# A selective state-space layer and a 34-expert feed-forward on one core: the loop rotated by three pairs, and the state-space work cut into half chunks

## The reference, cut to what matters

```python
# state-space layer, per batch; DI = 256 channels, DS = 16 states, L = 256 positions
x = einsum('ed,bld->bel', in_proj_w, hidden_states)      # hidden_states is ctx, 128 wide
u = silu(conv4(x) + conv_b)                               # causal convolution, 4 taps
x_dbl = einsum('ke,bel->bkl', x_proj_w, u)                # 8 rows dt_lo, 16 rows B, 16 rows C
delta = softplus(dt_proj_w @ dt_lo + dt_proj_b)
for t in range(L):
    state = state * exp(delta_t * A) + (delta_t * u_t) * B_t   # 256 channels x 16 states
    y_t = sum_n(state * C_t)
y = (y + D * u) * silu(z)                                 # z: the layer-normed input

# residual, layer norm, then the experts
probs = softmax(flat @ router_w + router_b); topk = top_k(probs, 6)
out = mean over 2 shared experts  of  relu(x @ w1 + b1) @ w2 + b2
    + sum over 32 routed experts of gate * (relu(x @ w1 + b1) @ w2 + b2)
```

## Time and profile before

| | |
|---|---|
| Median of 3 runs | 467.87 us (465.32 to 468.52) |
| The profiled execution's own time | 467.62 us |
| Its span, first to last instruction | 465.8 us |
| PE busy | 392.7 us (84%) |
| PEld busy | 345.1 us (74%) |
| DVE busy | 331.1 us (71%) |
| ACT busy | 244.6 us (53%) |
| POOL busy | 156.6 us (34%) |
| Chain that ended last, by engine | PE 52%, DVE 22%, issue 19%, ACT 4% |
| Mean granted TensorE clock | 0.952 of full speed |

### The profile page before, as it was taken

One profiled execution on the slowest core, in us unless ns is written; L12 is line 12 of the kernel. 1 busy time (PEld: TensorE's weight loads), 2 busy tenths in 40 slices (PEclk: granted clock), 3 DMA queues, 4 the chain that ended last, 5 costly groups with the idle time before them and its releaser, 6 DMA issues.

```text
span 465.8 us, 7761 instructions
## 1 busy us (share of the span) xinstructions
PE 392.7 (84%) x2610; PEld 345.1 (74%) x2610; DVE 331.1 (71%) x570; ACT 244.6 (53%) x536; POOL 156.6 (34%) x115
## 2 busy tenths in 40 slices
PE   1547655999777999899779999998879999999996
PEld 1225434888667898788668897887768998999996
DVE  3499965769999655579999565489999575444443
ACT  5565611884563252864553343856453445655662
POOL 0454440301455421202464321202465312444442
PEclk9998775899999999899998999899989999999999
DMA  5333483022121213122121224112212222332220
GB/s 187 90 90 97 131 225 149 23 52 83 49 69 39 77 58 113 52 60 68 45 68 45 68 59 125 52 48 65 61 52 67 58 66 91 90 91 78 85 68 24
DMA packets 18872, 36.29 MB, mean 78 GB/s; under 512 B 2082, under 2 KB 4898, under 8 KB 18756
## 3 DMA queue, kind: packets, MB, share of 16 engines
q1 hardware_dynamic: 18852, 36.04, 26.5%
HBM read 34.98 MB, written 1.05 MB: 77 GB/s over the span
## 4 chain that ended last, share of the span: by engine, by line
PE 52%; DVE 22%; issue 19%; ACT 4%; DVEq 1%; DMA 1%; SPq 0%; ACTq 0%
PE acc L401 22%; PE z L421 7%; DVE bu L659 7%; PE z L423 6%; PE z L422 6%; DVE bu L665 3%; DVE stage L739 3%; PE gb L430 3%; DVE pr L675 3%; DVE hl L751 1%; PE bb L340 1%; PE misc L335 1%; DVE cv L605 1%; PE cc L331 1%; PE misc L366 1%
## 5 line engine op out<-in xcount | busy, mean ns | idle before, releaser
L557 ACT ACTIVATE stage<-z,par 128x256 f32<-128x256 f32 x188 | 78.9, 470 | 143.8 <-PE z L423 143.7
L421 PE MATMUL z<-xh,w1l 128*128 (+1 forms) x376 | 116.9, 311 | 6.3 <-DVE stage L741 3.6
L808 POOL TENSOR_TENSOR w2l<-w,w2h 128x512 fp32r<-128x512 f32 (+1 forms) x51 | 68.8, 1351 | 143.2 <-ACT w2h L564 143.2
L423 PE MATMUL z<-xh,w1h 128*128 (+1 forms) x376 | 107.9, 287 | 0.0
L422 PE MATMUL z<-xl,w1h 128*128 (+1 forms) x376 | 107.8, 287 | 0.0
L739 DVE TENSOR_TENSOR stage<-stage,gb 128x512 f32<-128x512 f32 x88 | 59.9, 683 | 66.3 <-ACT stage L557 66.2
L790 POOL TENSOR_TENSOR ya<-ya,pr 128x512 f32<-128x512 f32 x42 | 55.6, 1346 | 120.6 <-DVE pr L675 120.6
L665 DVE TENSOR_TENSOR_SCAN bu<-dA,bu 128x512 f32<-128x512 f32 x64 | 81.3, 1310 | 3.4
L401 PE MATMUL acc<-stage,w 128*128 128x256 f32 x348 | 82.1, 379 | 0.0
L421 PEld LDWEIGHTS z<-xh,w1l 128*128 128x128 f32 x376 | 72.8, 194 | 11.5 <-DVE stage L741 4.7
L422 PEld LDWEIGHTS z<-xl,w1h 128*128 128x128 f32 x376 | 73.0, 194 | 0.8
(11 more groups left out here) (117 smaller groups left out, 512.8 us busy)
## 6 DMA issues: line engine op xcount, KB each, us to landing
w<-in_w SPq DMA_DIRECT2D x92, 256.0 KB, 2.7
stage<-in_w SPq DMA_DIRECT2D x11, 512.0 KB, 3.6
selg<-in_selg SPq DMA_DIRECT2D x1, 1056.0 KB, 8.4
x<-in_xT SPq DMA_DIRECT2D x4, 256.0 KB, 4.4
out<-x SPq DMA_DIRECT2D x4, 256.0 KB, 2.6
xr<-in_xr SPq DMA_DIRECT2D x1, 768.0 KB, 10.2
w<-in_w SPq DMA_DIRECT2D x4, 128.0 KB, 2.1
stage<-in_w SPq DMA_DIRECT2D x1, 384.0 KB, 4.2
```

The lines of the kernel that those rows point to most:

```text
L421: pe.matmul(z[p % 2][:, i, :], w1l[:, t, one], xh_, start=k == 0, stop=False)
L423: mm = pe.matmul(z[p % 2][:, i, :], w1h[:, t, one], xh_, start=False, stop=k == KD - 1)
L557: ins = act.activation(hg[:, p % 4, i, :], z[p % 2][:, i, :], ACT.Relu, bias=b1[:, t:t + 1])
L808: pool.tensor_tensor(w2l[:, p % 4, 0:n, :], w2[:, p % RING, 0:n, :], w2h[:, p % 4, 0:n, :].bitcast(F32), ALU.subtract).then_inc(S["w2l_don ...
```

## The change

The loop is rotated: one iteration now runs pairs 3 to 23 of batch i and then pairs 0 to 2 of batch i+1, so that the second layers of pairs 21 to 23 stand beside pairs 0 to 2 of the next batch. The loop has two iterations; the third such stretch and the last batch are written out. Each chunk is cut into two half chunks, one for each half k of the channels, one at each of the pairs 0 to 15, and the fold of a half chunk goes with it. The gate of z is spread over pairs 2 to 10. The steps ahead of the chunks are made for batch i+2, at pairs 14 to 23. The products for dt, B and C become one (`xall`). The second bias product moves to pair 4 (`B2_AT`). `SPLIT` has 12 pairs where it had 9, and now holds for batch 0 too. Scratch tiles are reassigned.

```diff
-CHUNKS = [(("chunk", c), at) for c, at in enumerate([6, 8, 9, 10, 11, 13, 14, 15])]
-FRONT = [("xin", 0), ("cv0", 0), ("stats", 0), ("taps", 0), ("rs1", 1), ("econv", 1), ("nb1", 1), ("uclip", 1),
-         ("usig", 3), ("u", 3), ("xdt", 4), ("dtl", 4), ("zsig", 3), ("zmul", 5), ("dt", 5), ("xbc", 5), ("split", 5), ("sp", 5),
-         ("delta", 5)]
-BACK = [("x1", 17), ("mean", 19), ("centre", 19), ("var", 20), ("r2", 20), ("norm", 21), ("xh", 23), ("logits", 23),
-        ("xl", 23), ("top", 23), ("ex", 23), ("gates", 23)]
-SPLIT = [0, 2, 3, 11, 12, 14, 19, 20, 21]
+UNITS = []
+for _c in range(NC):
+    UNITS += [(("B", _c), 2 * _c), (("C", _c), 2 * _c + 1)]
+    for _k in range(KD):
+        _u = 2 * _c + _k
+        UNITS += [(("decay", _c, _k), max(_u - 1, 0)), (("bu", _c, _k), _u), (("scan", _c, _k), _u),
+                  (("prod", _c, _k), _u), (("fold", _c, _k), _u)]
+ZGATE = [("stats", 2), ("rs1", 3), ("nb1", 4), ("zz", 5), ("ez1", 6), ("ez2", 7), ("ez3", 8), ("zmul", 10)]
+BACK = [("yfold", 16), ("x1", 17), ("mean", 18), ("centre", 18), ("var", 19), ("r2", 19), ("norm", 20), ("logits", 21),
+        ("xl", 21), ("top", 21), ("ex", 22), ("gates", 22)]
+NEXT = [("xin", 14), ("cv0", 15), ("taps", 16), ("econv", 17), ("uclip", 17), ("usig", 18), ("u", 19), ("xall", 20),
+        ("dtl", 20), ("split", 20), ("dt", 21), ("sp", 21), ("delta", 23)]
+OPEN = [[("xall", 1), ("dtl", 1), ("split", 1)], [("dt", 1), ("sp", 1), ("delta", 1)],
+        [(n, 1) for q in range(SKEW) for n, at in THIS if at == q]]
+SPLIT = [2, 4, 6, 8, 10, 12, 14, 17, 18, 19, 21, 22]
...
+            def beside(b, p, this=True, later=True):
+                return ([(n, b + 1) for n, at in THIS if this and at == p] +
+                        [(n, b + 2) for n, at in NEXT if later and at == p])
+
+            for name, b in HEAD:
+                step(name, b)
+            for p in range(SKEW):
+                pair(0, p, OPEN[p])
+            with eng.Fori(0, B - 2) as i:
+                for p in range(SKEW, NP):
+                    pair(i, p, beside(i, p))
+                for p in range(SKEW):
+                    pair(i + 1, p, beside(i + 1, p))
+                final(i)
...
+                elif name == "xall":
...
+                    for k in range(KD):
+                        mm = pe.matmul(cc[0:NXA, 0, :], xall[:, k, :], u[:, k, :], start=k == 0, stop=k == KD - 1)
...
+                elif name[0] == "bu":
+                    c, k = name[1:]
+                    if c == 0:
+                        dve.wait_ge(S["delta_done"], b + 1)
+                    else:
+                        dve.wait_ge(S["prod_done"], (b * NC + c - 1) * KD + k + 1)
+                    dve.wait_ge(S["b_ready"], b * NC + c + 1)
+                    dve.tensor_tensor(bu[:, k, :].rearrange("p (j l) -> p j l", j=2), bb[:],
+                                      du[:, k:k + 1, :].broadcast_to([P, 2, L]), ALU.mult).then_inc(S["bu_done"], 1)
+                elif name[0] == "scan":
+                    c, k = name[1:]
+                    nth = (b * NC + c) * KD + k + 1
+                    dve.wait_ge(S["bu_done"], nth)
+                    dve.wait_ge(S["da_ready"], nth)
+                    dve.tensor_tensor_scan(bu[:, k, :], dA[:, k, :], bu[:, k, :], 0.0, ALU.mult,
+                                           ALU.add).then_inc(S["scan_done"], 1)
```

More of the change, by code:

```diff
@@ L26 @@
 NC = NS // 2
+NBC = 3 * 2 * NS
+NXA = NBC + DR
 EPS = 1e-5
@@ L433, in pair @@
                     turn(b)
-                if more:
-                    beside(p, b_step, b + 1)
-                if p >= SKEW:
-                    second_layer(b, p - SKEW)
-                if more:
-                    beside(p, step, b + 1)
-            def end(b):
-                for p in range(NP - SKEW, NP):
-                    second_layer(b, p)
-            def b_then_step(name, b):
-                b_step(name, b)
-                step(name, b)
-            run(pe, pair, end, b_then_step)
+                for name, at in beside:
+                    step(name, at)
+                if exists(b, p, SKEW):
+                    second_layer(*before(b, p, SKEW))
+            run(pe, pair, nothing, step)
+            for p in range(NP - SKEW, NP):
+                second_layer(B - 1, p)
         @block.scalar
         def _(act):
-            me = Steps(act, act_step, 7)
+            fr, zs = Steps(act, act_front_step, 3), Steps(act, act_z_step, 3)
             act.preload_act_table_set("natural_log_exp_and_others")
@@ L550, in step, with pair @@
                     ins.then_inc(S["ex_done"], 1)
-            def pair(b, p, more):
-                if first("pair", b) or p == 0:
+            def pair(b, p, beside):
+                if first(b) and p < SKEW:
                     act.wait_ge(w1l_done, NW)
@@ L575, in upper_h @@
                 act.activation(hh[:, p % 4, 0:n], hg[:, p % 4, 0:n], ACT.Copy).then_inc(S["hh_done"], 1)
-            def end(b):
-                if split(b, NP - 1):
-                    upper_h(b, NP - 1)
-            run(act, pair, end, step)
+            run(act, pair, nothing, step)
+            upper_h(B - 1, NP - 1)
         @block.vector
         def _(dve):
-            me, own = Steps(dve, dve_step, 19), Steps(dve, dve_router_step, 15)
+            fr, zs = Steps(dve, dve_front_step, 8), Steps(dve, dve_z_step, 2)
+            bk, own = Steps(dve, dve_back_step, 8), Steps(dve, dve_router_step, 15)
             dve.memset(epsc[:], EPS).then_inc(const_done, 1)
@@ L742, in pair @@
                 ins.then_inc(S["hg_done"], 1)
-                if p and split(b, p - 1):
-                    lower_h(b, p - 1)
-                if more:
-                    beside(p, step, b + 1)
+                if exists(b, p, 1) and split(*before(b, p, 1)):
+                    lower_h(*before(b, p, 1))
+                for name, at in beside:
+                    step(name, at)
             def lower_h(b, p):
@@ L752, in lower_h, with final @@
                                   ALU.subtract).then_inc(S["hl_done"], 1)
-            def end(b):
-                if split(b, NP - 1):
-                    lower_h(b, NP - 1)
-                dve.wait_ge(S["acc_done"], b + 1)
+            def final(b):
+                dve.wait_ge(S["l2_done"], b * NP + NP)
                 dve.tensor_tensor(x1[:, b % 2], acc[:], x1[:, b % 2], ALU.add).then_inc(S["ot_done"], 1)
-            run(dve, pair, end, step)
+            run(dve, pair, final, step)
+            lower_h(B - 1, NP - 1)
+            final(B - 1)
         @block.gpsimd
@@ L800, in step, with pair @@
                                            ALU.add).then_inc(S["y_folded"], 1)
-            def pair(b, p, more):
-                if more:
-                    beside(p, step, b + 1)
+                elif first(b) and name in ("usig", "dtl", "sp"):
+                    split_w1(1)
+                elif name == "rest":
+                    split_w1(len(todo))
+            def pair(b, p, beside):
+                for name, at in beside:
+                    step(name, at)
                 if split(b, p):
```

453 lines of the change are left out of this document (224 added, 229 removed).

## The result

The changed kernel takes **488.39 us** (median of 4 runs, 486.23 to 494.24), the kernel before 466.6 (464.98 to 468.52): a ratio of 1.045, with a 95% interval of 1.0375 to 1.0524. It is slower by 4.5%, where 457 was forecast and 471 was the upper end.

The account below looks back on a forecast made before the run. DVE was taken to set the pace in the chunks and PE elsewhere, with a drain between batches. 78.3 + 104.3 + 97.4 + 93.8 + 77.6 + 3.7 = 455.1 span, so 457 us; range 437 to 471.

Parts of the forecast that it names:

- First z at 78.3: End of the prologue: first z product at 78.3 us, with 1.95 and 1.5 saved and 1.9 and some 0.6 coming back.
- The mechanism of the collision: In the chunks, POOL's fold delays hl by 0.70 and w2l delays a scan by 0.45: two pairs take 8.03, not 6.88.
- The border: Between batches: PE's clock near 1.00, rotation and spreading winning at most 45 us; PE waiting for relu would mean wrong in kind.
- The tail of a batch: Pairs 16 to 23, from DVE's last product to the next first z: 29.3 us in a looped batch.
- two inputs in SBUF: DVE operations with both inputs in SBUF don't run beside a POOL addition; those reading one input from PSUM aren't stretched.
- rival A: Collisions with POOL don't come or fall in DVE's slack: cycle 6.91, 433 us, or 445 for half; chance 0.19.
- The wait at `mean`: In a batch's tail, the taps on DVE stand before x1, so PE waits 4.1 us at mean.
- Batch 2: Without xall, dt, their 0.3 and 1.1 of the taps' wait, this batch takes 93.8 us.
- Batch 0: Its opening ends 20.8 us after first z, against 14.2 in a looped batch; taken as +6.9, giving 104.3.
- C: Rival: w2l, queued behind the fold, runs before the waiting hl, +0.85 a cycle, 18 us in all, 475; chance 0.12.
- B: Rival: waits written with loop registers cost 0.1 more on two steps of 16 half chunks, 465 to 469 us; chance 0.18.
- D: Rival: PE keeps its clock over the batch border, two or three us less a batch, 448 to 450; inside the forecast's 0.51.

Follow-up runs that it names:

- e1: Changed kernel with the load of ctxT issued after the fifth piece of first-layer weights (early load): 475.52 us, ratio 1.018 to the kernel before.
- e4: e1 with POOL's fold and w2l on 16 columns only, the rest of both left out: 447.71 us, ratio 0.9578 to the kernel before.
- e5: e1 with the back steps from mean to gates one pair later, and xh with them: 471.03 us, ratio 1.0098 to the kernel before.
- e8: e2, e5 and e7 together, with the early load of e1: 450.06 us, ratio 0.9667 to the kernel before.
- e10: e8 with an empty SPLIT, so no pair of batches 0 to 2 is split: 441.13 us, ratio 0.9485 to the kernel before.
- e9: Kernel before with only SPLIT shortened to 19, 20, 21: 455.91 us, ratio 0.9789 to the kernel before.
- e11: Kernel before with SPLIT empty: 458.51 us, ratio 0.9841 to the kernel before.
- e3: e1 with DVE making hl ahead of the gate product instead of behind it: 480.21 us, ratio 1.0308 to the kernel before.
- e2: e1 with pairs 2 to 14 taken out of SPLIT, leaving 17, 18, 19, 21, 22: 454.23 us, ratio 0.9741 to the kernel before.
- e7: e1 with whole chunks at the odd pairs instead of half chunks: 465.99 us, ratio 1.0002 to the kernel before.

## Why the prediction was wrong, point by point

- **"First z at 78.3": this step failed.** I counted what the prologue saved and what came back, and took the moved projection `xin` of batch 1 as free there. It was moved ahead of the last sum of states, and its input was the last transfer in SP's queue. I had noted neither, though both are to be read from the code and the trace of before. It is 11.7 of the 13.9 us that the first z came late, and so the largest single part of the 31; e1 shows it by itself (11.8 in the median), and none of the four rivals had it. The rest of the 13.9 is close to what `w1l` adds to two steps of the gate of z in the prologue, which I priced undisturbed. Without it 475 was left, still slower by 1.8%.
- **The mechanism of the collision was right, its reach too small.** `hl` +0.70 was 0.75 and the odd scan ended as forecast, from its start to the product 1.68 (228.47 - 226.79) against 1.69. But the even scan runs 1.30 and hands on after 1.41 against 1.24, half of it the 0.09 by which scan to product was under-priced everywhere. The cycle was 8.27 to 8.41, not 8.03: seven of them a batch, 1.7 to 2.7 us.
- **The border: a wait put at nothing.** The sum has no wait of PE for the final sum of the batch before. It was 2.78 and 2.79 us, the clock fell behind it to 0.74 and 0.72 where I had looked for 1.00 over the border, and DVE, which I never had waiting for relu, waited 1.95 and 1.85. I had named such a wait as a sign of being wrong, but for PE.
- **Where the batches missed.** Up to the DVE row behind the last product (167.36, 271.22, 372.66) the three batches took 75.2, 70.8 and 70.1 us against 75.0, 68.1 and 68.1; from there to the next first z 33.0, 31.4 and 31.8 against 29.3, 29.3 and 25.7. So the tail was longer than priced in every batch, and in batches 1 and 2 the part ahead of it too.
- **The tail of a batch: mis-sized by a new case of the same thing.** I applied the rule "two inputs in SBUF" to the chunks and not to the five `w2l` between pairs 17 and 22. There `uclip`, `u`, `xl` and steps of x1 last 1.5 to 1.8, about 1.1 us more each; `uclip` has a single input in SBUF, so that the rule as I had it would have missed it anyway. In batch 1 three of them add 3.2 us, and the wait at `mean` was 1.1 shorter than priced, which leaves the 2.1 by which this tail was longer. e4 takes the collisions of both parts away: 30 us, against the 24 of rival A.
- **The wait at `mean`: 4.1 predicted, 2.98, 2.97 and 4.34 measured.** Right in place and cause, but 2.97 is without a hit and 4.09 (e1) or 4.34 with hits on x1, which I hadn't counted. What it set off was missing: the clock falls behind it in two of the three batches, 1.7 and 2.8 us. e5, without the wait, has full-clock durations there and is 6.5 us faster.
- **Batch 2: 3.6 of savings that did not come.** With xall, dt and the taps gone, x1 itself was hit twice (1.87 instead of 0.88 at 375.53, 1.80 instead of 0.69 at 377.43), the wait at `mean` was the longest of the three and the clock loss the largest. So the 8.1 us are 2.0 up to the last product, and 6.1 of tail, 2.8 of them clock.
- **Batch 0** had the longer cycles too, and yet its part up to the last product was right to 0.2; so its opening was priced some 2 us too high. That was not taken apart; two misses of opposite sign met there.
- **The last batch and the end** were right to 0.3.
- **The rivals.** C, w2l before `hl`, did not happen: `hl` went first each time. A did not happen in the changed kernel, and e4 shows what it would have given. B: the gap from `bu` to scan is 0.03 in the loop too (226.79 against 226.08 + 0.68); only scan to product has a tenth more, and it has it in straight code as well (1.33 in batch 2, from 310.04), so B fell. D, a clock kept over both borders, is seen in e8 and e10 only.
- **The splits.** I priced three more splits a batch as nearly free, with their collisions inside the cycle. On average a split beside a chunk costs about 1 us net (21 us for 7 in 3 batches, all taken away at once), although it saves PE 0.33. e9 shows the same sign in the kernel before, 9.75 us for six, and e11 the opposite one for its last three.

## What to carry to other kernels

When a step is moved earlier in an engine's queue, look up when its input is issued, not only what the step costs: the transfer that nobody used to need is the one that was put last. A precomputing engine that shares a port with the engine that sets the pace isn't free when it is idle most of the time (POOL is busy 36% of the span in e1); count for each of its operations which one of the other engine it will meet, over the whole batch and not only in the stage you study. And before a reordering is judged, take away the work that collides with it: the same rotation came out at +4.5% or at -2.6% by one load and the list of splits.

## What the hardware showed that I had not expected

- Where two engines contend, moving one operation by 0.6 us changed who was hit and hardly how long two pairs took: 8.33 a cycle in e1, 8.17 in e3.
- After a wait of PE at `mean` of 1.64 us or less, in e2, e4, e5 and e8, the products behind it had full-clock durations (mean 1.12, second layer 1.89). After 3.78 us or more, in e1, e3, e7 and the changed kernel, they fell to half clock each time. Around 3 us both were seen: 2.98 gave half and 2.97 full in the changed kernel, 2.99 half in e1, 3.24 full and 3.25 half in e3. The length of the wait alone doesn't decide it: in e5 PE waits 1.78 us at the variance in batch 0 and its granted clock is 0.72 over about the next 6 us, and 1.77 us in batch 1, where it is 1.00. What decides no run isolates; it stays open. Two rows of PE in e1, of the second kind:

```profile
266.78 1.68 PE L406 MATMUL misc<-x,meanw 128*128 x4 [4.09 <-DVE x L733]
268.26 3.06 PE L447 MATMUL acc<-stage,w 128*128 128x256 f32 x8
```
